# Filler products on TensorE left out at the border of two stages of a two-layer kernel

## What is computed

```python
x = first layer's result
xn = layernorm(x)
# attention: 16 heads of 8, no mask
q, k, v = split(xn @ w_qkv)
attn = softmax(q @ k^T / sqrt(128))
a = (attn @ v) @ w_out
# experts: 8, the best 2 of each token, hidden size 512
score = relu(xn @ rw1 + rb1) @ rw2 + rb2
gate = softmax over the best 2 scores
f = sum_e gate_e * (relu(xn @ W1[e] + b1[e]) @ W2[e] + b2[e])
out = x + a + f
```

## Time and profile before

| | |
|---|---|
| runs | 1141.26, 1136.08, 1139.98 us (median 1139.98) |
| profiled execution | 1139.31 us |
| its span | 1137.6 us, mean granted TensorE clock 0.95 |
| PE busy | 974.3 us (86%) |
| DVE busy | 909.8 us (80%) |
| ACT busy | 787.7 us (69%) |
| POOL busy | 561.9 us (49%) |
| products on `ident` into PHh, PW (whole run) | 104 and 64 records |

### The profile page before, as it was taken

One profiled execution on the slowest core, in us unless ns is written; L12 is line 12 of the kernel. 1 busy time (PEld: TensorE's weight loads), 2 busy tenths in 40 slices (PEclk: granted clock), 3 DMA queues, 4 the chain that ended last, 5 costly groups with the idle time before them and its releaser, 6 DMA issues. The chain is left out here.

```text
span 1137.6 us, 23649 instructions
## 1 busy us (share of the span) xinstructions
PE 974.3 (86%) x9302; PEld 519.0 (46%) x9302; DVE 909.8 (80%) x1006; ACT 787.7 (69%) x859; POOL 561.9 (49%) x571
## 2 busy tenths in 40 slices
PE   5787778889778799999987688998999999989897
PEld 3522222233467344333333578634645465555533
DVE  7888888899777999999996867677686667476857
ACT  3689999999764899999997532432366656555574
POOL 6088888528637558888886523407720000000172
PEclk9889999999989999999999688997799999999999
DMA  8891011012188212222210784000314344432121
GB/s 292 229 376 37 31 36 33 22 39 67 39 226 193 77 58 72 71 73 73 74 55 34 203 218 118 4 1 22 98 49 130 94 120 139 122 102 84 38 59 45
DMA packets 102597, 109.56 MB, mean 96 GB/s; under 512 B 11893, under 2 KB 87121, under 8 KB 98769
## 3 DMA queue, kind: packets, MB, share of 16 engines
q1 hardware_dynamic: 93492, 87.67, 26.8%
q0 software_dynamic: 7424, 20.20, 5.9%
q10 hardware_dynamic: 1571, 0.20, 0.1%
HBM read 62.29 MB, written 42.59 MB: 92 GB/s over the span
## 5 line engine op out<-in xcount | busy, mean ns | idle before, releaser
L262 DVE SCALAR_TENSOR_TENSOR ring<-AD,PT 128x1808 f32<-128x1808 f32 (+15 forms) x128 | 282.2, 2221 | 28.1 <-PE LG L985 27.3
L985 PE MATMUL LG<-ring,lred 128*32 128x456 f32 (+15 forms) x2048 | 237.2, 583 | 0.0
L268 POOL DMA_INDIRECT ys<-rows,goali x80 | 162.1, 2027 | 72.3 <-DVE rows L869 49.4
L2362 DVE TENSOR_REDUCE MX<-SS 128x2 f32<-128x1024 f32 x119 | 144.5, 1218 | 55.6 <-PE SS L2079 55.5
L2292 ACT ACTIVATE EX<-SS 128x1024 f32<-128x1024 f32 x128 | 130.3, 1031 | 79.3 <-PE SS L2079 78.8
L925 ACT ACTIVATE ring<-ring 128x3680 f32<-128x3680 f32 (+15 forms) x47 | 161.2, 3429 | 3.6 <-DVE ring L262 3.6
L1010 PE MATMUL SD<-DSf,eyes 99*32 99x456 bf16 (+15 forms) x1280 | 96.3, 377 | 66.4 <-ACT ring L930 63.1
L931 ACT ACTIVATE ring<-ring 128x1824 f32<-128x1824 f32 (+15 forms) x80 | 145.8, 1822 | 0.0
L1996 POOL DMA_INDIRECT XN<-ys,sloti x16 | 16.4, 1024 | 246.8 <-PE SS L2089 242.2
L778 POOL DMA_INDIRECT xs<-rows,sloti x64 | 121.7, 1902 | 30.5 <-issue 19.2
L985 PEld LDWEIGHTS LG<-ring,lred 128*32 128x32 f32 x2048 | 61.5, 111 | 99.1 <-issue 76.2
(11 more groups left out here) (434 smaller groups left out, 1720.6 us busy)
## 6 DMA issues: line engine op xcount, KB each, us to landing
w1s<-in_L_ffn_W SPq DMA_DIRECT2D x39, 256.0 KB, 3.0
w2s<-in_L_ffn_W SPq DMA_DIRECT2D x39, 256.0 KB, 3.0
band<-Z SPq DMA_DIRECT2D x8, 1024.0 KB
xl<-xs SPq DMA_DIRECT2D x20, 272.0 KB, 3.1
xs<-Z SPq DMA_DIRECT2D x5, 1024.0 KB, 9.7
w1s<-w1d SPq DMA_DIRECT2D x80, 64.0 KB
w2s<-w2d SPq DMA_DIRECT2D x80, 64.0 KB
ring<-band SPq DMA_DIRECT2D x12, 384.0 KB, 9.5
```

The source lines that it names most:

```text
L262: return v.scalar_tensor_tensor(out=tile[:, s, :, t0:T], in0=AD[:, s, :, j + t0:j + T], scalar=extra, in1=AD[:, s, :, PAD + t0:PAD + T], o ...
L268: pool.indirect_dma_start(ys0[:, :], bass.IndirectOffsetOnAxis(ap=goali[:, 4 * n + a:4 * n + a + 1], axis=0), yo[:, n % 2, a, :], None, bo ...
L985: mm = pe.matmul(LG[32 * b:32 * b + 32, par, s, t0:T], lred[:, s, n % 4, :], ring[:, slot, s, b, t0:T], start=(n % 4 == 0), stop=(n % 4 == 3))
L2362: v.tensor_reduce(MX[:, t, p // 2, hh:hh + 2], pairs_of(b, name), AX.X, ALU.max).then_inc(freed[slot], 1)
```

## The change

Three groups of filler products are left out, all in the second layer's PE program: `occupy(8)` ahead of the third bias set and `occupy(3)` behind each of the last seven steps of the first stage; `occupy(5)` ahead of that stage's `t0`; and the pair of products behind the back scores in steps 1 to 18 of the second stage wherever no value products stand (steps 1 to 7, 12 to 14 and 16). That is 34 products and 22 products. No wait and no other instruction is changed.

```diff
         def bias_out(i):
             pe.wait_ge(gt_sb, 4)
-            if i == 2:
-                occupy(8)
             if i >= 2:
                 emptied(pe, 1, "k1")
...
             if n == BIAS_STEPS[1] + 3:
                 pe.wait_ge(b2_sb, 1)
-            if n >= BIAS_STEPS[1] + 3:
-                occupy(3)
...
                     b, name = fronts[s][n]
-                    if name == "t0" and s == 0:
-                        occupy(5)
                     if name == "t1" and s == B - 1:
                         occupy(5)
...
                             values(Q, i - 6)
-                        if s == 1 and 1 <= n < START_STEP and (Q == 0 or i >= NT):
-                            keep_busy(pe, PYy[:, 0, :], ident, 2)
                         if s == B and i >= NT and not spread(Q):
                             occupy(2)
```

## The result

| | before | changed |
|---|---|---|
| median, in runs of one session | 1140.58 us (9 runs, 1136.08 to 1141.26) | 1144.67 us (9 runs, 1142.78 to 1149.39) |
| ratio | | 1.0041, 95% interval 1.0024 to 1.0057 |
| profiled execution | 1139.31 us | 1144.67 us |
| its span, mean clock | 1137.6 us, 0.95 | 1142.6 us, 0.93 |
| PE busy | 974.3 us | 967.0 us |

The changed kernel is 4.1 us slower by the medians, 0.41%. The forecast was 1142.7 us and "within 0.5%", the range 1138 to 1148: the time lies in it. PE is busy 7.3 us less and the kernel takes longer.

The account below looks back on a forecast made before the run. PE's groups were taken to fill most of the chain that ended last, with fillers on it in places. The terms -0.75 + 0.6 + 1.1 + 2.5 = +3.4 us on 1139.31 gave 1142.7 us, range 1138 to 1148.

Parts of the forecast that it names:

- The choice of the clock: Without fillers, the low clock was taken at the first stage's end (gain 0.75 us, 4.3 if high) and near 835.
- End of the first stage, -0.75: Without 34 products, the second stage's first score starts at 807.6 instead of 808.35: gain 0.75 us.
- the fourth bias set: End of the first stage: this set runs 797.6 to 799.5, then score 36 to 800.3, its maximum to 801.5.
- Steps 0 to 8, +0.6: Second stage: steps 0 to 2 run at 1.91 us instead of 1.62, low from the start: +0.6 us.
- the removal itself gains nothing: First steps of the second stage: ACT's loop covers the filler pairs, so leaving them out gains nothing at either clock.
- Steps 8 to 12, +1.1: Value products from step 8: clock rises about 3 us into them, before 1.5; +1.1 us, ends 0 and +1.9.
- The second fall, +2.5: Steps 12 to 14, scores alone: clock falls at about 835, delaying `sel` and later values; +2.5 us, ends 0 and +3.2.
- The rest unchanged: Behind 846 nothing is changed and PE is busy at clock 1.00, so the difference is carried through.
- The signs: Trace checks: first score of the second stage within 1 us of 808, first expert transpose some 3 us later than 845.7.
- The clock stayed high: Rival: clock high without fillers through first-stage end and steps 1 to 8; -7.0 us, 1132.3 us; chance 0.08.
- high for the turns: Rival: clock rises in the turns' 16 records, second turn saves 0.9; +1.9, 1141.2 us; chance 0.13.
- stay low into the experts: Rival: value products of steps 8 to 11 don't lift the clock; +7.9, 1147.2 us; chance 0.27.

Follow-up runs that it names:

- early_pairs: Against the kernel before, only the 7 filler pairs of steps 1 to 7 of the second stage left out; median 1146.91 us, ratio 1.0066.
- late_pairs: Against the kernel before, only the 4 filler pairs of steps 12 to 14 and 16 of the second stage left out; median 1145.55 us, ratio 1.0046.
- end_only: Against the kernel before, only the 34 fillers at the end of the first stage left out; median 1139.86 us, ratio 1.0006.
- hold3: Kernel before with fillers added in the second stage: 4 at step 0, 3 instead of 2 behind the back scores; median 1142.80 us, ratio 1.0020.

## Why the prediction was right

Point by point, by its own steps:

- *The choice of the clock.* At both places where I had to choose between the levels the low one came: 0.50 from 785.9 to 826.9, and again from 833.7. This choice carries the forecast; with the other one it would have been -7.0 us and the wrong side.
- *End of the first stage, -0.75.* Right in sign, too small: -1.8 and -2.2 in the two executions. The step that was wrong is the fourth bias set, which I put ahead of score 36 in series (797.6 to 799.5, then the score). In the timeline score 36 starts at 797.21 while that set runs from 796.36 to 798.26: the two overlap, and the maximum of score 36 starts at 798.34, right behind DVE's addition (lines below). Counted from the last projection that is 0.8 us earlier than forecast; the way from the end of the maximum to the turn took 0.8 us for 0.9, and the turns 3.68 for 3.8.
- *Steps 0 to 8, +0.6, "the removal itself gains nothing".* Right: exponentials 1.91 us apart from the first step on (806.40, 808.31), the first of them 0.3 later behind its score. early_pairs confirms the cover. One reading was off: from 811.7 to 825.4 the kernel before has six pairs, not seven; the first of the seven stands at 810.52.
- *Steps 8 to 12, +1.1.* +1.4: two steps of 2.6 us instead of one and a half of 2.4. early_pairs shows that the missing pairs are what delays the rise. At the low clock with values, PE alone sets the step: eight records took 1.93 us, not the 1.76 of the earlier trace rows, in which the clock rose before their end.
- *The second fall, +2.5.* +2.7. It fell at 833.7, forecast about 835; the product with `sel` took 2.08 us, forecast 2.07. Within it two errors offset each other: up to the exponential of step 16 it lost 1.2 us (forecast 0.8), and the values of steps 17 and 18 1.3 (forecast 1.4), the second of them partly at the high clock. late_pairs shows that four pairs are what held it.
- *The rest unchanged.* Behind the stretch not so in the first execution (+3.2), so in the second (0.0); ahead of it 1.1 us were gained in the first, where the change can't reach. The medians put the total at +4.1, the stretch gives 2.9 and 2.7. The 1.3 us between them are within what the rest moves from one execution to the next (1082.0 to 1085.8 us for this kernel), and I can't say whose they are. The sum put this term at nothing, and what covered it was the width of the range.
- *The signs.* Two of them missed: the first score of the second stage came at 805.45, not within 1 us of 808 (1.1 us of it from ahead of the stretch, 1.0 from the end of the first stage), and the first expert transpose at 847.55, 1.8 us later by the clock of the trace, 2.9 when counted from the last projection.
- *The rivals.* The clock stayed high in neither execution of the changed kernel. It was high for the turns in one of two, worth 0.2 us and not the 1.5 that I gave it, since it fell again before step 1. It did not stay low into the experts: the value products of steps 8 to 10 lifted it at 826.9. On the Trainium skill's rule about idle gaps (page "TensorE: Matmul & The Clock Gate", section "Why this matters for your kernels"): the trace does not agree. The clock fell at 833.7, and in the 6.8 us at the high clock ahead of that PE's longest wait was 1.1 us; from 805.5 to 821.6 the longest was 1.1 us too, and it was low throughout.

DVE of the changed kernel, for the end of the first stage:

```profile
797.74 0.68 DVE L2366 TENSOR_TENSOR ACC<-ACC,PW 128x512 f32<-128x512 f32 x1
798.34 1.23 DVE L2354 TENSOR_REDUCE MX<-SS 128x2 f32<-128x1024 f32 x1
```

## What to carry to other kernels

Filler products are priced by two things apart: the place where they stand in PE's queue, and the clock that the work behind them gets. Price each group separately. Those under another engine's loop cost nothing by themselves and can hold the clock or bring its rise forward: here the 8 products of steps 12 to 16 are worth some 3 us and the 14 of steps 1 to 7 some 1.2. Those on the path can cost more than they give back: with the 34 products at the end of the first stage that piece took about 2 us more, though in 8 of 10 executions they kept the clock high once it had risen. And measure such a change by a stretch between two fixed instructions, the first of them ahead of the edit, in more than one execution and cut into pieces, since the rest of this kernel moves more than the effect and a clock that is up by chance in one piece can hide a loss in the next.

## What the hardware did that I had not expected

- PE being busy without a pause does not lift the clock in this kernel, where the work is score products of 32 rows with a pair of fillers: 13.70 of 13.70 us at 0.50 in late_again, 16.93 of 17.10 in end_only. With four fillers at step 0 and three per step instead of two it stayed at 1.00 for 35 us, with PE busy 33.71 us in the first and 33.73 us in the second execution of hold3.
- An execution's time outside the stretch ranged from 1081.1 to 1090.3 us over 14 profiled executions, though the instructions there are the same. Even the part ahead of the stretch, which no edit here can reach, ranged from 785.8 to 793.7 us. Medians of small edits in this kernel can therefore differ by more than the edits explain: early_pairs, +6.5 us by its median and at most 1.4 in the stretch.
